# The last expert layer's end: where the last block's rows are gathered, when they are added, and how the result is stored

## What is computed

```python
def _moe_forward(...):                 # 512 rows at a time, H = 256, 16 experts, 4 of them per row
    tidx, tw = _route(x, router_weight, e_bias)
    g = jnp.einsum('th,eih->tei', x, gate_w)
    u = jnp.einsum('th,eih->tei', x, up_w)
    h = jax.nn.silu(g) * u
    yo = jnp.einsum('tei,ehi->teh', h, down_w)
    routed = jnp.einsum('te,teh->th', combine, yo)
    shared = _mlp(hidden_states.reshape(-1, H), sh_gate_w, sh_up_w, sh_down_w)
    return (routed + shared).reshape(orig_shape)
...
x = x + jnp.tanh(g_ffn[1]) * _L1_ffn_ref(_layernorm(x, axis=-1), ...)
```

## Time and profile before

| | |
|---|---|
| Median of 3 runs | 1926.91 us (1920.95 to 1927.06) |
| The profiled execution, its own time | 1910.97 us |
| Its span, first to last instruction | 1908.7 us |
| TensorE's mean granted clock | 0.945 |
| Busy in the span: PE, PEld (weight loads) | 1651.9 us (87%), 1256.1 us (66%) |
| VectorE (DVE), ScalarE (ACT), GpSimd (POOL) | 1188.1 us (62%), 1005.9 us (53%), 763.4 us (40%) |
| DMA | 256.99 MB, 135 GB/s on average |

### The profile page before, as it was taken

The page is one execution under the profiler, slowest core; times in us unless marked ns, Lnnn a source line. Parts: engine busy times, 40 slices in busy tenths (PEclk is TensorE's granted clock), DMA queues, the critical chain, the costliest instruction groups (busy, mean ns, idle before and its releaser), DMA issues. The chain is left out here.

```text
span 1908.7 us, 44330 instructions
## 1 busy us (share of the span) xinstructions
PE 1651.9 (87%) x16920; PEld 1256.1 (66%) x16920; DVE 1188.1 (62%) x2667; ACT 1005.9 (53%) x1744; POOL 763.4 (40%) x932
## 2 busy tenths in 40 slices
PE   4699999758999999999995899999886898888885
PEld 3355666437888888888883566665643777776753
DVE  4678887735555565565566788777762556345546
ACT  4377877635445444444433456645544576555541
POOL 2155657875310101000036334423651535565534
PEclk9699999978999999999997999989997999999898
DMA  9753333214645544544224434423243456677523
GB/s 288 208 117 68 72 60 68 57 41 133 203 150 196 172 139 167 195 158 135 67 84 107 99 80 79 71 55 58 76 125 144 164 200 233 232 235 250 190 90 121
DMA packets 297700, 256.99 MB, mean 135 GB/s; under 512 B 198047, under 2 KB 270155, under 8 KB 296216
## 3 DMA queue, kind: packets, MB, share of 16 engines
q1 hardware_dynamic: 271256, 168.84, 32.5%
q0 software_dynamic: 26240, 85.32, 13.4%
HBM read 102.98 MB, written 107.74 MB: 110 GB/s over the span
## 5 line engine op out<-in xcount | busy, mean ns | idle before, releaser
L1643 PE MATMUL ps<-m_xT,m_w_halves 128*128 128x256 f16 x3360 | 413.9, 273 | 2.2 <-issue 2.2
L1643 PEld LDWEIGHTS ps<-m_xT,m_w_halves 128*128 128x128 f16 x3360 | 329.4, 98 | 41.4 <-issue 2.8
L1158 ACT ACTIVATE a_probs<-ps 128x1024 f32<-128x1024 f32 (+1 forms) x256 | 234.8, 917 | 183.8 <-PE ps L995 181.9
L1662 PE MATMUL ps<-m_w_halves,m_hiddenT 128*128 128x256 f16 x1680 | 229.8, 273 | 5.1 <-DVE m_hiddenT L1758 4.6
L1274 POOL TENSOR_TENSOR a_probs<-a_probs,a_half_above 128x512 f32<-128x512 f32 x128 | 162.3, 1270 | 157.2 <-ACT a_probs L1158 156.6
L1719 ACT ACTIVATE m_hiddenT<-m_hidden 128x256 f16<-128x256 f32 x280 | 116.6, 416 | 197.6 <-DVE m_hidden L1755 191.6
L1758 DVE TENSOR_TENSOR m_hiddenT<-m_hidden,m_hiddenT 128x256 f16<-128x256 f32 x280 | 119.2, 426 | 135.1 <-ACT m_hiddenT L1719 130.7
L1610 POOL DMA_DIRECT2D expert_out<-m_y x40 | 28.9, 722 | 434.8 <-DVE m_y L1738 432.2
L2162 ACT ACTIVATE m_rowsT<-ps 128x1024 f16<-128x1024 f16 x112 | 115.9, 1035 | 154.0 <-remote 93.8
L1357 DVE TENSOR_REDUCE a_qT<-ps 128x4 f16<-128x1024 f32 x128 | 156.5, 1223 | 51.1 <-PE ps L1006 50.2
L1662 PEld LDWEIGHTS ps<-m_w_halves,m_hiddenT 128*128 128x128 f16 x1680 | 163.5, 98 | 26.9 <-DVE m_hiddenT L1758 7.2
(11 more groups left out here) (319 smaller groups left out, 3070.3 us busy)
## 6 DMA issues: line engine op xcount, KB each, us to landing
routed<-m_zeros POOLq DMA_DIRECT2D x32, 768.0 KB
r_space<-routed SPq DMA_DIRECT2D x48, 512.0 KB
routed_out<-m_y SPq DMA_DIRECT2D x48, 512.0 KB
r_w_load<-in_L_w SPq DMA_DIRECT2D x24, 896.0 KB
dispatched<-r_xT SPq DMA_DIRECT2D x10, 1024.0 KB, 6.6
expert_out<-m_y POOLq DMA_DIRECT2D x40, 256.0 KB
a_ctx_in<-in_ctx SPq DMA_DIRECT2D x32, 256.0 KB
m_experts_load<-in_L_experts SPq DMA_DIRECT2D x18, 384.0 KB, 3.5
```

The lines of the kernel that those rows point to most:

```text
L1158: A(pr[:, g % 2, 2 * jp:2 * jp + 2, :], SC[:, :, 0:SPAN], ACT.Exp, scale=1.0 / math.sqrt(DH)).then_inc(asem["ex"], 1)
L1643: last = mm(psum[:, v % HB, m * CH:(m + 1) * CH], wh[:, u, ws_, m, d_ * F0 + f_ * P:d_ * F0 + (f_ + 1) * P], xT[:, q % XB, xs_ * KT + d_, ...
L1662: last = mm(psum[:, 4 + 2 * (q % 2) + t, 0:D], hT[:, hs_, f_, t * P:(t + 1) * P], wh[:, u, ws_, 2, f_ * D:(f_ + 1) * D], start=f_ == 0 and ...
```

## The change

Three things change. The last block's gathered rows (tiles 24 to 31) go to a view of `wh` instead of `yb`, each tile in a place of its own; tiles 28 to 31 no longer wait for `used`, and have semaphores of their own, `got_late`. `COMBINE_BEHIND` names pair 12 behind job 4, 13 behind 5, 14 behind 6 and 15 behind 7, and `combine(15)` behind everything is gone, so `add_job(7)` is VectorE's last step. The last block leaves in three stores instead of one: tiles 24 to 27 (512 KB) behind pair 13 and job 6, tiles 28 and 29 (256 KB) behind pair 15 and the first half of job 7's addition, tiles 30 and 31 behind its second half.

```diff
--- before.py
+++ after.py
@@ -1813,6 +1813,14 @@
         with nc.sbuf_tensor("m1_xn", [P, RT, D], F32) as xn, nc.sbuf_tensor("m1_xT32", [P, KT, RT * P], F32) as xT:
             pass
         yb = sb("gathered", [P, GB, K1, D], F32)
+        late_rows = wh.rearrange("p s e n -> p (s e n)")[:, 0:RT * K1 * D * 2].bitcast(F32)\
+            .rearrange("p (t k d) -> p t k d", t=RT, k=K1)
+        LATE = (RG - 1) * RT
+
+        def gathered(nt):
+
+            return late_rows[:, nt - LATE] if nt >= LATE else yb[:, nt % GB]
+
 
         w_in = w1_in
         xn_ready, xT_done, xT_out = sem("m1_xn_ready"), sem("m1_xT_done"), sem("m1_xT_out")
@@ -1823,6 +1831,13 @@
         y_done, y_out, used = sem("m1_y_done"), sem("m1_y_out"), sem("m1_combined")
         y_sent = [sem(f"m1_y_sent{u}") for u in range(YB)]
         stored = sem("stored")
+        got_late = [sem(f"m1_got_late{u}") for u in range(NT - LATE - GB)]
+
+        def rows_gathered(nt):
+
+            if nt >= LATE + GB:
+                return got_late[nt - LATE - GB], 16 * K1
+            return got[nt % GB], GOT0 + 16 * K1 * (nt // GB + 1)
 
         H0 = CHUNKS0 * FT0
         X0 = [16 * 2 * len(range(u, CHUNKS0, XB)) for u in range(XB)]
@@ -1833,7 +1848,7 @@
         PACED = (("scatter", 1, 0, 8, 32), ("scatter", 2, 9, 0, 32), ("gather", 0, 17, 0, 8), ("scatter", 3, 19, 0, 32),
                  ("gather", 0, 27, 8, 32), ("gather", 1, 33, 0, 32), ("gather", 2, 41, 0, 28))
         PAIR_AT = {20: 0, 30: 1, 32: 2, 34: 3, 36: 4, 38: 5, 40: 6, 42: 7, 44: 8, 46: 9, 48: 10}
-        COMBINE_BEHIND = {1: 11, 3: 12, 4: 13, 5: 14}
+        COMBINE_BEHIND = {1: 11, 2: 12, 3: 13, 4: 14, 5: 15}
         turned = psum[:, 4, :].bitcast(F16)
         rows_turned = psum[:, 5, :].bitcast(F16)
 
@@ -1890,9 +1905,14 @@
                         store(r - LAG)
                     if r == 42:
                         finish(0)
-                for b in range(1, RG):
+                for b in range(1, RG - 1):
                     finish(b)
-                sp.wait_ge(stored, 16 * RG)
+                for pairs, job, half in ((2, 6, 1), (4, 7, 0), (4, 7, 1)):
+                    sp.wait_ge(used, RT * K1 * (RG - 1) + 2 * K1 * pairs)
+                    sp.wait_ge(y_out, 2 * place_of_job(job) + half + 1)
+                    t0, t1 = (LATE, LATE + QT) if job == 6 else (LATE + QT + 2 * half, LATE + QT + 2 * half + 2)
+                    sp.dma_start(out_dram[:, t0:t1, :], x[:, t0:t1, :]).then_inc(stored, 16)
+                sp.wait_ge(stored, 16 * (RG + 2))
 
             @block.gpsimd
             def _(pool):
@@ -1913,11 +1933,11 @@
                     for j in range(first, end):
                         t, k = j // K1, j % K1
                         nt = b * RT + t
-                        if nt >= GB and k == 0:
+                        if GB <= nt < LATE + GB and k == 0:
                             pool.wait_ge(used, 2 * K1 * ((nt - GB) // 2 + 1))
                         pool.indirect_dma_start(
-                            yb[:, nt % GB, k, :], None, eo[b],
-                            bass.IndirectOffsetOnAxis(ap=rows[:, nt, k:k + 1], axis=0)).then_inc(got[nt % GB], 16)
+                            gathered(nt)[:, k, :], None, eo[b],
+                            bass.IndirectOffsetOnAxis(ap=rows[:, nt, k:k + 1], axis=0)).then_inc(rows_gathered(nt)[0], 16)
 
                 for k in range(2, PAIR_STEPS):
                     pair_newton(pool, 1, 7, k)
@@ -2280,11 +2300,11 @@
                 def combine(pair):
                     for t in range(2):
                         nt = 2 * pair + t
-                        dve.wait_ge(got[nt % GB], GOT0 + 16 * K1 * (nt // GB + 1))
+                        dve.wait_ge(*rows_gathered(nt))
                     for k in range(K1):
                         for t in range(2):
                             nt = 2 * pair + t
-                            V.scalar_tensor_tensor(x[:, nt, :], yb[:, nt % GB, k, :], gw[:, nt, k:k + 1], x[:, nt, :],
+                            V.scalar_tensor_tensor(x[:, nt, :], gathered(nt)[:, k, :], gw[:, nt, k:k + 1], x[:, nt, :],
                                                    ALU.mult, ALU.add).then_inc(used, 1)
                         dve.wait_ge(used, 2 * K1 * pair + 2 * (k + 1))
 
@@ -2352,7 +2372,6 @@
                     if j - JA in COMBINE_BEHIND:
                         combine(COMBINE_BEHIND[j - JA])
                 add_job(JA + JB - 1)
-                combine(15)
         stack.close()
 
     attention(0)
```

## The result

The changed kernel takes 1930.19 us (median of 11 runs, 1924.51 to 1936.70), the kernel before, beside it, 1925.81 us (11 runs, 1918.85 to 1930.97). The ratio is 1.0034, with a 95% interval of 1.0019 to 1.0049: slower, where 0.5% faster was forecast.

What follows compares the result with a forecast made beforehand. Bound at the end: PE-VectorE handoffs, then bare last additions and store, with late releases beside gathers. -3.63 (additions) - 2.32 (store) - 3.8 (last release) = -9.75 us, giving 1917.2 us; range 1911.1 to 1924.9.

Steps and rivals of the forecast that it cites:

- The additions: VectorE's tail after job 7 loses one combine call, -3.63 us; the new call behind job 4 costs 0, bound +0.3.
- the 6.15 us of cover: VectorE's idle hole ahead of 1868.54, behind job 4, taken to hide the new 3.62 us call; without it 1.1 us cost.
- The store: Tail behind the last addition: last store 256 KB instead of 1 MB, 2.58 us in place of 4.90, -2.32 us.
- The gathers: POOL's last 24 gathers run on without pause at 1.25 us each; rows arrive in time, so combine's wait costs 0.
- The margin of 2.8 us: Pair 15's gathered rows land by 1887.8 and are wanted by VectorE at 1890.64, 2.8 us to spare.
- The 1.01 us for a gather beside additions: A POOL gather beside VectorE additions takes 1.01 us, against 0.95 quiet; the margins still hold.
- The last release: VectorE's late start on job 7's down products becomes prompt once gathers end earlier: -3.8 us, bounds 0 and -6.9.
- The release behind job 4's down products: ScalarE takes the transposes there 1.9 us after PE's recorded end; listed as late, with no term in the sum.
- the release behind job 5's down products: Gathers now run beside them; 2.7 us late there costs 0, bounds 0 and +1.5 us.
- Rival 3: Slower: six PE handoffs from 1867 to 1888 each released 3.35 us late, +7.0 us, 1934 us; chance 0.07.
- The sum: Additions, store and last release together: -9.75 us on the span, taken off the median for 1917.2 us, 0.5% less.
- rival 4: Job 6's and job 7's down products are both released promptly: -12.85 us, 1914.1 us; chance 0.08.

Runs made afterwards that it cites:

- the copies: The change with its last 32 indirect gathers replaced by plain copies, against the kernel before: 0.9930 issued by SP, 0.9905 issued by POOL, on slower chips.
- the second chip: A slower chip, kernel before 1913.84 us; the unaltered change 1.0051 against it, also three stores alone 0.9984 and moved additions alone 1.0002.
- the fifth chip: A quicker chip, kernel before 1836.91 us; the unaltered change measured 0.9970 against it, and with plain copies issued by POOL 0.9958.
- the two repeats: The unaltered change run again on two slower chips against the kernel before: 1.0051 and 1.0043.
- the fourth chip: A slower chip, kernel before 1911.43 us; against it the unaltered change 1.0043, the change with gathers in groups of four 0.9941, with SP's copies 0.9930.

## Why the prediction was wrong

**The additions.** -3.63 us forecast, -3.67 measured. The new call behind job 4 was taken as free for the 6.15 us of cover. In after no cost of it shows (+0.1 us from job 4's to job 5's additions), because a late release stands beside it. That cover was itself a late release, and where none stands there, it is gone. Job 4's to job 5's additions take 9.15 us in the change on a quicker chip, where they took 7.93 with only the gathers freed, and 9.16 and 9.15 us with the copies on slower chips. That is 1.2 us, near the 1.1 us that the prediction gave for a lost cover.

**The store.** -2.32 us forecast, -2.21 and -2.32 measured (4.90 to 2.69 us in the first profiles, 4.93 to 2.61 on the second chip). Alone, with 512 KB at the end, -1.6 us. The rate of the row was right.
By the fit of the Trainium skill (DMA: Bandwidth & Descriptors, Anatomy of one DMA — SWDGE (gpsimd) path) the step from 1 MB to 256 KB was an estimated 1.8 us. The page gives that fit for DMAs that GpSimd issues, and these stores are issued by SP. The trace has 2.2 to 2.3, so the row was the better guide.

**The gathers.** 1.25 us each, right on both kinds. They were in time on slower chips. The margin of 2.8 us was wrong on quicker ones, where they came 2.34 us late, because it was counted against jobs that ran late. The 1.01 us for a gather beside additions was too little: beside `combine(14)` the profile of before itself has 1.09 and 1.13, and the change on the fifth chip has up to 1.23, where quiet ones take 0.95.
By the Trainium skill's rule of what excludes what (SBUF — State Buffer, Who interferes with whom) each could have lost 0.48 us more. The 0.06 to 0.28 us measured speak against it for indirect gathers.

**The last release.** -3.8 us forecast, with a bound of -6.9. Measured -7.2 between job 6's and job 7's additions, since the gathers were over before job 6 began to wait. They were over because job 5 had been held for 21 us, which was not foreseen, so the size is luck. That late releases go where no gathers are under way was read right.

**The release behind job 4's down products** is the step that failed. The prediction lists it with 1.9 us ("3.0, 4.1 and 1.9 us here") and gives it no term in the sum, as if it kept that size. Yet the change lets the gathers run on past this very release, where in before they stopped near 1865.6. A term was given only to the release behind job 5's down products: "With a release 2.7 us late there [...] So 0, with bounds of 0 and +1.5". Job 5's down products came at 1912.20, when the gathers were over, and nothing was late there. What was held back was the release of job 7's turned rows behind job 4's down products, and it cost 20.9 us, and 21 to 22 in the two repeats.

I had taken the lateness of a release as a size, 1.9 to 4.1 us. The rows suggested something else, had I read their ends and not their lengths: ScalarE went on at 1867.00, behind a row of gathers that ended on POOL near 1865.6, and VectorE at 1898.47, behind one that ended at 1896.33. In these cases, as at 1905.85 in after, the release came 1.4 to 4.4 us behind the end of the row. In before only the last microsecond of the row was left when the transposes came (1864.54), so little of this showed. It is not a strict rule. ScalarE went on at 1888.58 in before and at 1879.53 in after in the middle of a row, and before's own row of 16 gathers held releases back by 4.1 and 3.0 us only. What lets a release through is open. Rival 3 came nearest, with 0.07 and 1934 us, but with five more waits of 3.35 us each. It was one wait, nearly as long as the row lasts.

**The sum.** By the table: +1.9 + 20.9 + 0.1 - 7.2 - 3.7 - 2.2 = +9.8 us against the -9.75 forecast; the medians moved by +4.4 us and the ratio gives 6.5. With the gathers in fours, the fourth chip has 50.9 us from job 2 to the end where the profiles of before have 60.0, or -9.1 us, near the forecast. Without indirect gathers in the way it is 46.4 to 46.6 us on both kinds of chip, 13.5 us less than before on slower ones, which is nearer rival 4's 12.85. On a quicker chip the kernel before was never profiled, so there the split into parts can't be checked. In the chances of "faster", rival 4 should have counted with its whole 0.08 and not 0.07.

## What to carry to other kernels

Before gathers or scatters are let run on without a wait, look for engines that go on long after PE's records end, and compare the moment at which they go on with the end of the row of indirect DMAs: if they fall together, a wait that seemed to cost POOL 10 us may be what let PE's results through, as it was here. In this kernel it paid to keep such rows at four, with a wait on the consumers' own progress between them: the paced kernel is 0.45 to 0.59% faster than the kernel before on both kinds of chip, where the unpaced one is 0.3% faster on one and 0.3 to 0.5% slower on the other. And a cover that consists of a wait without a known cause isn't a cover.

## What the runs showed of the hardware

The same kernel takes 1837 to 1838 us on three chips, 1911 to 1914 us on three others and 1926 us in the runs of the result. On the quicker ones no wait on an unnamed releaser showed in any profile's ScalarE rows, on the slower ones 24 to 32 in its taking of turned rows, the longest 28.0 us. While a row of gathers runs on a slower chip, PE can issue one to four matmuls at a time, with starts often 0.7, 1.4 or 2.1 us apart, and the engines that wait for its results mostly see them when the row is over. PE's granted clock was at its half level from 1887 to 1910 in after, where PE worked one or two matmuls at a time. That doubles the 0.23 us of a hidden matmul (2.75 us for twelve in the earlier trace rows) to 0.46; the lone ones are recorded at 0.58. A plain copy of 128 rows of 1 KB costs POOL 0.5 us where the gather costs 1.25 with its gap.
